# Attention with a feed-forward layer: the transposes of the probabilities at the end of each step, two PSUM banks lent in other steps, and two rotation halves a step later

## The reference

```python
q, k, v = (einsum('btm,mhd->bthd', x, w) for w in (w_aq, w_ak, w_av))
q, k = rope(q), rope(k)                          # halves rotated by cos and sin
s = einsum('bihd,bjhd->bhij', q, k) / 128        # causal mask, then
p = softmax(s)
r = einsum('bhij,bjhd->bihd', p, v) -> einsum('bihd,hdm->bim', ., w_ao)
x = layernorm(x + r)
h = silu(x @ w1 * s1) * (x @ w2 * s2)
h = gelu(h @ h1 * sg1); h = gelu(h @ h2 * sg2)
out = layernorm(x + h @ w3 * s3)
```

## Time and profile before

| | |
|---|---|
| median of 3 runs | 1065.2 us (1064.57 to 1065.36) |
| the profiled execution's own time | 1065.99 us |
| its span, first to last instruction | 1064.2 us |
| PE busy | 997.1 us (94%) |
| DVE, ACT, POOL busy | 820.6, 593.3, 539.6 us (77, 56, 51%) |
| mean granted PE clock | 0.98 of full |

### The profile page before, as it was taken

One profiled execution on the slowest core, in us unless ns is written; L12 is line 12 of the kernel. 1 busy time (PEld: TensorE's weight loads), 2 busy tenths in 40 slices (PEclk: granted clock), 3 DMA queues, 4 the chain that ended last, 5 costly groups with the idle time before them and its releaser, 6 DMA issues. The chain is left out here.

```text
span 1064.2 us, 19686 instructions
## 1 busy us (share of the span) xinstructions
PE 997.1 (94%) x5648; PEld 860.2 (81%) x5648; DVE 820.6 (77%) x1803; ACT 593.3 (56%) x1255; POOL 539.6 (51%) x536
## 2 busy tenths in 40 slices
PE   3799999999999999999999999999839999999995
PEld 3688888898888889888888888888728878788784
DVE  5888888888888888887888888788555677486744
ACT  3566666665666666566666666666434252433521
POOL 4666767776676776677677666767250101000000
PEclk9899999999999999999999999999969999999998
DMA  8433233432322123323222222221020000000000
GB/s 282 150 127 74 61 80 97 124 99 56 75 69 69 49 59 100 70 61 79 59 49 59 61 70 68 72 59 40 1 80 1 1 1 21 1 20 0 1 20 21
DMA packets 33292, 66.16 MB, mean 62 GB/s; under 512 B 5457, under 2 KB 6993, under 8 KB 32209
## 3 DMA queue, kind: packets, MB, share of 16 engines
q1 hardware_dynamic: 30400, 58.62, 21.0%
q10 hardware_dynamic: 2832, 6.82, 1.7%
HBM read 24.26 MB, written 7.34 MB: 30 GB/s over the span
## 5 line engine op out<-in xcount | busy, mean ns | idle before, releaser
L703 POOL TENSOR_SCALAR probs<-probs,inv_sum 128x128 f32<-128x128 f32 (+7 forms) x256 | 191.1, 747 | 232.4 <-DVE inv_sum L621 231.8
L534 ACT ACTIVATE pT<-psum 128x512 fp32r<-128x512 f32 (+3 forms) x384 | 173.9, 490 | 144.0 <-PE psum L401 141.9
L308 PE MATMUL psum<-pT,vals 128*128 128x512 f32 (+3 forms) x1152 | 242.6, 351 | 1.6 <-DVE rT L663 1.6
L522 ACT ACTIVATE probs<-psum,neg_max 128x128 f32<-128x128 f32 (+7 forms) x256 | 190.5, 744 | 80.2 <-DVE neg_max L615 79.8
L615 DVE TENSOR_REDUCE neg_max<-psum 128x1 f32<-128x128 f32 (+7 forms) x256 | 191.2, 747 | 54.8 <-PE psum L392 53.6
L631 DVE TENSOR_TENSOR pT<-psum,pT 128x512 fp32r<-128x512 f32 (+3 forms) x384 | 200.7, 551 | 32.3 <-ACT pT L534 25.3
L308 PEld LDWEIGHTS psum<-pT,vals 128*128 128x128 f32 x1152 | 187.7, 189 | 23.9 <-DVE pT L631 1.7
L401 PE MATMUL psum<-ident,probs 128*128 128x128 f32 x1152 | 173.7, 277 | 12.9 <-POOL probs L703 12.2
L883 PE MATMUL ps<-hid,w 128*128 128x512 f32 x768 | 181.3, 396 | 0.0
L708 POOL TENSOR_TENSOR swapped<-by_cos,swapped 128x512 f32<-128x512 f32 x128 | 164.7, 1298 | 14.2 <-DMA swapped<-by_sin 14.2
L883 PEld LDWEIGHTS ps<-hid,w 128*128 128x128 f32 x768 | 143.7, 188 | 34.5
(11 more groups left out here) (77 smaller groups left out, 1195.3 us busy)
## 6 DMA issues: line engine op xcount, KB each, us to landing
swapped<-by_sin SPq DMA_DIRECT2D x256, 128.0 KB, 2.3
w_stage<-qk_split SPq DMA_DIRECT2D x30, 256.0 KB, 2.7
wv_stage<-v_split SPq DMA_DIRECT2D x15, 256.0 KB, 2.7
x_split<-ffn_raw ACTq DMA_DIRECT2D x2, 1024.0 KB, 5.8
ffn_raw<-g SPq DMA_DIRECT2D x2, 1024.0 KB, 8.0
x_moving<-x_split SPq DMA_DIRECT2D x2, 1024.0 KB, 5.1
out<-y SPq DMA_DIRECT2D x4, 512.0 KB, 2.6
raw_x<-xT SPq DMA_DIRECT2D x3, 512.0 KB, 11.6
```

The lines of the kernel that those rows point to most:

```text
L308: ins = nc.tensor.matmul(out_ap, left[a], right[b], start=first and i == 0, stop=last and i == 2)
L522: nc.scalar.activation(probs[:, ib % 4, :width].rearrange("p (h c) -> p h c", h=halves), score_ps[:, ib % 2, :halves, :half], ACT.Exp, bia ...
L534: nc.scalar.activation(pT[chunk][:, 0, 4 * f:4 * f + n_blocks, (ib % 4) * P:(ib % 4 + 1) * P], bank("t", head[1], nth)[:, :n_blocks * P].r ...
L703: nc.gpsimd.tensor_scalar(p, p, inv_sum[:, n:n + 1], 1.0, ALU.mult, ALU.mult).then_inc(probs_ready[0], 1)
```

## The change

Within a step, PE now does the transposes last, after projections and products with values; ACT and DVE likewise take a fill out after their work on values (and DVE after the rotation products). `plan_banks` lists the uses in the new order. Bank 1 is lent from step 5 on (to step 0), bank 3 in steps 7, 0 and 1. The rotation of tiles 2 and 3 is a step later throughout: sums in steps 5 and 6 (before: 4 and 5), high parts in steps 6 and 7 (before: 5 and 6), low parts in steps 7 and 8 (before: 6 and 7). POOL now makes low parts ahead of sums within a step. No instruction is added or removed.

```diff
-SUM_STEP = (2, 2, 4, 5)
-HIGH_STEP = (3, 3, 5, 6)
-LOW_STEP = (3, 4, 6, 7)
+SUM_STEP = (2, 2, 5, 6)
+HIGH_STEP = (3, 3, 6, 7)
+LOW_STEP = (3, 4, 7, 8)
...
-LEND1 = (6, 7, 0)
-LEND3 = (1, 2)
+LEND1 = (5, 6, 7, 0)
+LEND3 = (7, 0, 1)
...
-            after = ([("t", off, FIRST_FILL[s] + k) for k in range(FILLS_OF[s])]
-                     + [("qk", off + 1, j) for j in range(NQK) if QK_STEP[j] == s]
-                     + [("v", 0, c) for c in range(NV) if V_STEP[c] == NI * off + s])
+            after = ([("qk", off + 1, j) for j in range(NQK) if QK_STEP[j] == s]
+                     + [("v", 0, c) for c in range(NV) if V_STEP[c] == NI * off + s]
+                     + [("t", off, FIRST_FILL[s] + k) for k in range(FILLS_OF[s])])
...
@@ PE, step @@
-                if exists(head):
-                    transpose_probs(head, s)
                 for target, j in rope_tasks(head, s, QK_STEP):
                     project_qk(step_on(target, -1), j)
                 for c in v_tasks(head, s):
                     project_v(head[0], b, c)
...
                 if s in PV1_PIECES and exists(step_on(head, -1)):
                     attend(step_on(head, -1), 1, PV1_PIECES[s])
+                if exists(head):
+                    transpose_probs(head, s)
@@ ACT, step @@
                 for target, j in rope_tasks(head, s, HIGH_STEP):
                     roped_high(target, j)
+                for c in v_tasks(head, s):
+                    values_high(head[0], c)
                 if exists(head):
                     transposed_high(head, s)
-                for c in v_tasks(head, s):
-                    values_high(head[0], c)
@@ DVE, step @@
-                if exists(head):
-                    transposed_low(head, s)
                 for target, j in rope_tasks(head, s, QK_STEP):
                     rope_products(target, j)
                 for c in v_tasks(head, s):
                     values_low(head[0], c)
+                if exists(head):
+                    transposed_low(head, s)
@@ POOL, step @@
+                for target, j in rope_tasks(head, s, LOW_STEP):
+                    roped_low(target, j)
                 for target, j in rope_tasks(head, s, SUM_STEP):
                     rope_sum(target, j)
-                for target, j in rope_tasks(head, s, LOW_STEP):
-                    roped_low(target, j)
```

## The result

The changed kernel takes 1092.3 us (1091.22 to 1093.22, 4 runs) against 1065.3: 1.0253 times as long, 95% interval 1.0236 to 1.0271. It is slower, by 27 us, as forecast; the forecast was 1104.5 us, 12 too high. PE's busy time has hardly changed (996.4 us, 91% of 1091.4, for 997.1), nor has that of DVE and POOL (822.7 and 538.9 us); ACT's fell to 581.2 us. The new time is waiting.

A forecast was written before the change was run, and what follows sets the result against it. PE sets the pace, so only its waits can be won. Border +34.5, value tile 1 +10.4 and gain -5.6 make +39.3 on 1066.0, 1105.3; that execution stands 0.8 above the median: 1104.5 us, range 1078 to 1112.

The forecast's parts named there:

- The bank at the border: Between pairs, PE's first q/k projection waits for bank 4 until DVE's low part of fill 11: 15 x 2.3 = 34.5 us.
- theory A: Expectation for e1_cyc: the border wait is only a matter of which bank; time falls by 31 to 1061 us.
- Value tile 1: First head, step 5: it takes bank 1 and waits for exp of block 6; 16 x 0.65 = 10.4 us.
- The gain: Waits won back in the second head's tail and step 2: 16 x 0.35 = 5.6 us, at most 22.
- the tail: Second head from the end of step 3: 9.45 us against 9.65; of 1.2 won, 1.0 comes back.
- The chain: Second head's tail, timed link by link across ACT, DVE, POOL and PE from the end of step 3.
- bank 1 at the scores of step 2 in the second head: Bank 1 waits for q/k tile 0's product instead of tile 1's; 0.15 us won.
- (a): Border: ACT is not held by tile 3, the wait is near 1.1 us; 1086 us; chance 0.20.
- (b): Faster: tail's waits go altogether, value tile 1 doesn't wait, border costs its least; 1060 us; chance 0.07.
- (d): Half the waits are taken up by slack behind them; 1071 to 1077 us; chance 0.05.
- (e): The waits delay each other further, in the first head too; above 1112 us; chance 0.03.
- (c): The clock falls in the new waits at 15 borders, 43 us more; 1147 us; chance 0.05.

The follow-up runs named there:

- e1_cyc: The changed kernel with the bank plan made to go round: planned four times over, each from the banks' last uses in the pair before; 1072.6 us.
- e8_high_only: The changed kernel, but in step 7 ACT makes tile 3's high part after its copies of the fills; 1078.7 us.
- e4_cyc_v: e1_cyc, and value tile 1 takes no lent bank; 1078.2 us.
- e6_add_banks: e1_cyc, plus DVE adding a head's first half in its own step 7; value tile 1 takes no lent bank, next projection's first q/k tile bank 1; 1055.4 us.
- e9_step2_early: e7_high_last with PE's transposes of step 2 put back between the scores and the projections; 1067.5 us.
- e2_rope_back: The changed kernel with the three rotation tables for tiles 2 and 3 as before the change; 1101.2 us.
- e10_best_rope_back: e7_high_last with the rotation of tiles 2 and 3 a step earlier, as before the change; 1080.2 us.
- e7_high_last: e6_add_banks, and in step 7 ACT makes tile 3's high part after the fills' copies; 1047.4 us, the fastest version.

## Why the prediction was right, and where its sizes were off

**The bank at the border** was the right step. Predicted: 15 waits, 1.1 to 2.3 us, taken at 2.3, for 34.5 us. Measured: 15 waits, 2.21 us longer steps, 33 us. e1_cyc shows by removal that the plan is its cause, e8_high_only that about half is ACT held by tile 3. The lower end, 1.1, was measured at 1.02.

**What lay under it** was missing from the prediction: it named nothing that was late behind it. Bank 7 and exp of block 1 were late too, hidden behind the bank (e1_cyc: 0.7 and 0.3 us of step length). This did not touch the forecast, since these waits lay under a longer one (step 1 is 2.42 us in the changed kernel), but theory A's expectation for e1_cyc was wrong by 11 us for it.

**Value tile 1**: predicted 0.65 us in 16 pairs, 10.4 us; measured 0.59 in the step's length, 9.4 us, of which the view of the waits shows 0.36 as idle time. Another bank gives back 0.46 of it (e4_cyc_v, e6_add_banks); the other 0.13 is not explained. The place and the cause were right, the size nearly.

**The gain** is the term that was mis-sized: 0.35 us a pair, 5.6 us, against 0.85 in the second head and 0.40 in the first, 20 us in all, nearly the upper bound of 22; a pair takes 47.65 us and not 48.6. I put it too low in three places.

First, the tail: predicted 9.45 us, measured 9.23 (401.45 to 410.68). By the table's medians, which start from 9.73, it is 0.48 us gained, where the prediction had 0.20. The chain held link by link up to the end of exp of block 6 (predicted 4.16 after the end of step 3; the rows give 404.46 + 1.10 - 401.45 = 4.11), but I had DVE's adding and low parts end at 4.5, and its reciprocal started at 405.74, 4.29.

Second, bank 1 at the scores of step 2 in the second head: I estimated 0.15 from a wait of the weight loads; step 1 became shorter by 0.21. e4_cyc_v, where bank 1 waits for tile 1's product again, confirms the place: step 1 is the one that grows (3.20), and step 2 stays at 4.08.

Third, steps where I looked for no gain since no idle time was shown: in the first head step 2 is 0.22 and step 6 0.18 shorter, and in the second head step 2 is 0.14 shorter. In the trace of the kernel before, transposes between two groups of products leave longer distances around them that no busy or idle figure shows, because a matmul's length overlaps the next (0.39 us long, 0.23 apart). By the starts of single matmuls, as medians, block 2's transposes come 0.30 us after the last score matmul in the first head and 0.15 in the second, and in both heads the products behind them have one distance of 0.31 where 0.23 is usual. The 0.30 is, I take it, a short wait for the probabilities; no such wait shows in the second head, whose step 2 was still 0.14 longer. How much the mere alternation costs stays open: e9_step2_early could not separate it.

The total came out closer than its terms: the gain was 14 us too small, the border and value tile 1 together 2 us too dear, and some 4 us that the prediction did not have, of the clock and the kernel's ends, took back part. That the measured time lies 12 us and not 17 below the forecast is luck to that extent.

**The part not weighed** was the coupling. The prediction priced the later rotation as a loss at the border alone and never asked what the tail would be with the early one. e2_rope_back and e10_best_rope_back show that the late transposes need it: without it, 1.3 us a pair are lost in step 6.

**Rivals.** (a), with ACT not held, did not occur in the changed kernel, but its mechanism is e8_high_only's. (b) did not occur. (d) and (e) did not. (c), the falling clock, occurred at 2 of the 15 borders, below.

## What to carry to other kernels

When a plan for a loop body gives out buffers by least recent use, start it from the state at the body's end, not from empty: the first use of a body is the neighbour of its last. When an order of work is moved on one engine, list for each of its consumers what now stands ahead of it in every in-order queue (here ACT's high part and DVE's addition), and move these as well. The change was a loss of 27 us as it stood and, with the banks and these two put right, a gain of 18. And a wait taken away shows the next one: before promising its length as a gain, work out when each later thing on that engine would be ready.

## What the runs showed of the hardware

The clock. PE's waits of 2 us at the borders left the granted clock at full (1.00, 2.4 GHz) in 13 of 15 cases, and in two it fell to 0.50, its 1.2 GHz level, shortly after. In e2_rope_back and e8_high_only, where the border wait is 1.0 us, it is 1.00 throughout from 60 to 730 us. PE's timeline and the windows of the changed kernel at the first of these:

```profile
76.75 2.10 PE L308 MATMUL psum<-x_moving,w_stage 128*128 128x512 f32 x6 [1.99 <-DVE pT L631]
```

```profile
69.00:76.70 7.70, 5.62 (x41) 4.88 (x40) 5.32 (x15) 5.83 (x14) 6.57 (x7) 1.00 0.00 0
77.90:81.10 3.20, 3.20 (x10) 2.52 (x9) 3.15 (x7) 0.85 (x3) 1.00 (x2) 0.50 0.36 85
81.30:89.00 7.70, 7.70 (x44) 6.82 (x43) 5.35 (x10) 3.36 (x8) 4.13 (x5) 1.00 0.43 97
```

The two pairs took 49.23 and 49.27 us in place of 47.65, so the cost was 1.6 us each and not the 2.9 of rival (c). At the end of attention a wait of 1.04 us followed by one of 2.26 left the clock at 0.74 on average for the 24 last products, which took 6.42 us where they had taken 4.86 after a wait of 1.62 us:

```profile
793.10:799.60 6.50, 6.42 (x24) 5.24 (x24) 0.00 (x0) 0.00 (x0) 0.00 (x0) 0.74 0.01 3
```

The last wait's length does not decide this alone. In e7_high_last it is 1.57 us, shorter than the 1.62 before, and follows one of 1.03 where the kernel before has one of 0.45. The products take 6.42 us there, at the same mean clock. The kernel before:

```profile
764.32 1.09 PE L401 MATMUL psum<-ident,probs 128*128 128x128 f32 x8 [0.45 <-POOL probs L703]
```

And e7_high_last, PE's timeline and the window:

```profile
745.49 1.09 PE L408 MATMUL psum<-ident,probs 128*128 128x128 f32 x8 [1.03 <-POOL probs L714]
748.16 6.42 PE L315 MATMUL psum<-pT,vals 128*128 128x512 f32 x24 [1.57 <-DVE pT L642]
```

```profile
748.10:754.60 6.50, 6.42 (x24) 5.26 (x24) 0.00 (x1) 0.00 (x0) 0.00 (x0) 0.74 0.01 3
```

So waits of 2 us at the borders were usually free of this penalty, but not always, and a shorter one close behind another was not. The Trainium skill (TensorE: Matmul & The Clock Gate, Part 1) says that half rate is the default and that PE's activity releases the full one; the two falls after waits of 2 us, with PE busy all through the slow stretch and the clock full again behind it, agree with that.
